# Edge counts from 16-bit keys, lanes first, and one product for attributes and squares

## The reference, cut to what matters

```
out_deg = segment_sum(ones, src, num_segments=12500)      # how many edges leave each node
h       = concatenate([x[row], edge_attr], axis=1)        # edge_attr: 400000 x 32
m       = h.mean(0)
v       = ((h - m) ** 2).mean(0)                          # batch norm over the edges
```

## Time and profile before

| what | value |
|---|---|
| median of three runs | 26533.92 us |
| the profiled execution, time | 26542.53 us |
| the profiled execution, span | 26540.7 us |
| VectorE busy, whole span | 58% |
| TensorE busy, whole span | 57% |
| GpSimd busy, whole span | 59% |

### The profile page before, as it was taken

The page is one execution under the profiler, slowest core; times in us unless marked ns, Lnnn a source line. Parts: engine busy times, 40 slices in busy tenths (PEclk is TensorE's granted clock), DMA queues, the critical chain, the costliest instruction groups (busy, mean ns, idle before and its releaser), DMA issues. The chain is left out here.

```text
span 26540.7 us, 456722 instructions
## 1 busy us (share of the span) xinstructions
PE 15258.6 (57%) x102440; PEld 9002.1 (34%) x102441; DVE 15401.4 (58%) x31597; ACT 5213.2 (20%) x13760; POOL 15770.5 (59%) x16798
## 2 busy tenths in 40 slices
PE   7555555566666689951000000024777777787777
PEld 5344444333333388920000000023333333333333
DVE  9666666656566644431111118985666666666666
ACT  4211111111111144410000000000222222222222
POOL 0377777677777744416777777721555555555554
PEclk9655555555555555555555555555888888888888
DMA  2466666433333345403333332212444444444444
GB/s 66 117 173 172 173 173 173 112 68 69 68 69 68 63 148 154 131 15 86 92 92 92 92 92 70 71 46 66 111 111 111 110 110 110 110 111 110 110 110 104
DMA packets 2864906, 2738.33 MB, mean 103 GB/s; under 512 B 1320271, under 2 KB 2226317, under 8 KB 2861906
## 3 DMA queue, kind: packets, MB, share of 16 engines
q1 hardware_dynamic: 2297486, 2308.45, 31.4%
q0 software_dynamic: 412544, 241.53, 6.1%
q10 hardware_dynamic: 153668, 172.93, 2.6%
HBM read 2173.30 MB, written 537.93 MB: 102 GB/s over the span
## 5 line engine op out<-in xcount | busy, mean ns | idle before, releaser
L2225 POOL DMA_INDIRECT rows_x<-x_table,index x3125 | 2974.6, 952 | 3538.4 <-DMA index<-in_src 2765.6
L742 POOL DMA_INDIRECT rows<-split_table,index x3125 | 2999.6, 960 | 1937.5 <-DMA index<-in_src 1008.2
L1624 POOL DMA_INDIRECT rows_dram<-rows,place_now x3125 | 3026.4, 968 | 1484.9 <-issue 952.3
L858 POOL DMA_INDIRECT rows<-x_table,index x3125 | 3279.8, 1050 | 1021.3 <-issue 952.1
L2339 DVE TENSOR_TENSOR second<-banks,h 128x768 f32<-128x768 f32 x2500 | 1944.8, 820 | 1597.8 <-PE banks L2494 1597.8
L1552 DVE TENSOR_REDUCE rows<-banks 128x108 f32<-128x324 f32 x1250 | 490.7, 434 | 3467.3 <-DMA rows_dram<-rows,place_now 3450.7
L1564 PE MATMUL banks<-row_pieces,hot_turned 128*128 x3125 | 394.1, 291 | 3604.6 <-DMA hot_turned<-turned_dram 3602.0
L2331 DVE TENSOR_TENSOR first<-banks,h 128x768 f32<-128x768 f32 x2500 | 1937.9, 818 | 259.3 <-issue 138.3
L550 PE MATMUL banks<-counts,low_turned 128*128 128x98 f32 x6250 | 1793.3, 435 | 80.3 <-ACT counts L538 47.3
L550 PEld LDWEIGHTS banks<-counts,low_turned 128*128 128x128 f32 x6250 | 1600.9, 314 | 205.4 <-issue 175.1
L2469 PE MATMUL banks<-u_turned,w_tensor 32*128 32x384 f32 (+1 forms) x10000 | 1565.0, 501 | 145.3 <-DVE second L2339 145.3
(11 more groups left out here) (480 smaller groups left out, 33841.6 us busy)
## 6 DMA issues: line engine op xcount, KB each, us to landing
key_row<-dst_rows SPq DMA_DIRECT2D x1250, 320.0 KB, 3.5
h<-hidden_dram SPq DMA_DIRECT2D x1250, 320.0 KB, 4.2
acc_moved<-dst_rows SPq DMA_DIRECT2D x625, 320.0 KB
src_row<-in_src_rows SPq DMA_DIRECT2D x625, 320.0 KB
hot_turned<-turned_dram SPq DMA_DIRECT2D x1250, 160.0 KB, 3.2
hot_dram<-onehot SPq DMA_DIRECT2D x625, 160.0 KB
turned_dram<-hot_turned SPq DMA_DIRECT2D x625, 160.0 KB
a_dram<-a ACTq DMA_DIRECT2D x625, 160.0 KB
```

Of the source, the lines that this page charges most:

```text
L742: nc.gpsimd.indirect_dma_start(out=m["rows"][j][:, t * SPLIT:(t + 1) * SPLIT], out_offset=None, in_=m["split_table"], in_offset=bass.Indir ...
L858: nc.gpsimd.indirect_dma_start(out=m["rows"][j][:, t * C2:t * C2 + F], out_offset=None, in_=m["x_table"], in_offset=bass.IndirectOffsetOnA ...
L1624: nc.gpsimd.indirect_dma_start(out=m["rows_dram"], out_offset=bass.IndirectOffsetOnAxis(ap=m["place_now"][j][:, t:t + 1], axis=0), in_=m[" ...
L2225: nc.gpsimd.indirect_dma_start(out=m["rows_x"][j][:, t * F:(t + 1) * F], out_offset=None, in_=m["x_table"], in_offset=bass.IndirectOffsetO ...
```

## The change

The edges' keys `low` get a bfloat16 copy, `low_half`, and the ramp is written out once as bfloat16 with each value five times in a row, `ramp_each`. Both operands and the result of the two comparisons are then bfloat16. The tiles `hot_low` and `hot_high` are laid out with the lanes innermost: value r, lane t is column 5*r + t. The comparison therefore runs over rows of five; the key is read as the same row of five again and again, the ramp and the result in one run. The counting products read one lane of such a tile, which is every fifth element, for the weights and for the moving operand.

The squares are written behind the attributes in one tile `attr[j]` of 320 columns, and one float32 product of ones with the 320 columns takes the place of the two with 160. Both sums lie in bank 1. The waits are as they were. Values 0 to 127 are exact in bfloat16.

```diff
@@ SyncE @@
-                    sp.dma_start(m["attr"][j][:, :], m["edge_attr"][:, bass.ds((SLOTS * i + j) * T * F, T * F)]
+                    sp.dma_start(m["attr"][j][:, 0:T * F], m["edge_attr"][:, bass.ds((SLOTS * i + j) * T * F, T * F)]
@@ ScalarE @@
-                    nc.scalar.square(m["attr_square"][j][:, :], m["attr"][j][:, :]).then_inc(s["squared"], 1)
+                    nc.scalar.square(m["attr"][j][:, T * F:], m["attr"][j][:, 0:T * F]).then_inc(s["squared"], 1)
@@ VectorE @@
             nc.vector.tensor_copy(m["ident_half"][:, :], m["ident"][:, :])
+            link(nc.vector.tensor_copy(m["low_half"][:, :], m["low"][:, :]))
+            by_lane = lambda tile: tile.rearrange("p (r t) -> p r t", t=T)
+            link(nc.vector.tensor_copy(by_lane(m["ramp_each"][:, :]), rep(m["ramp"][:, :], 2, T)))
             with dve.Fori(0, ITERS) as i:
                 for j in range(SLOTS):
                     dve.wait_ge(s["counted"][j], ONE + i)
                     cols = bass.ds((SLOTS * i + j) * T, T)
-                    nc.vector.tensor_tensor(cut(m["hot_low"][j][:, :], t=T), rep(m["low"][:, cols], 2, P),
-                                            rep(m["ramp"][:, :], 1, T), ALU.is_equal)
-                    nc.vector.tensor_tensor(cut(m["hot_high"][j][:, :], t=T), rep(m["high"][:, cols], 2, NB),
-                                            rep(m["ramp"][:, 0:NB], 1, T), ALU.is_equal).then_inc(s["hot"], 1)
+                    nc.vector.tensor_tensor(by_lane(m["hot_low"][j][:, :]), rep(m["low_half"][:, cols], 1, P),
+                                            by_lane(m["ramp_each"][:, :]), ALU.is_equal)
+                    nc.vector.tensor_tensor(by_lane(m["hot_high"][j][:, :]), rep(m["high"][:, cols], 1, NB),
+                                            by_lane(m["ramp_each"][:, 0:T * NB]), ALU.is_equal).then_inc(s["hot"], 1)
...
-            nc.vector.tensor_reduce(m["attr_sum"][:, F:2 * F], by_feature(m["ps"][2]), AX.X, ALU.add)
+            nc.vector.tensor_reduce(m["attr_sum"][:, F:2 * F], by_feature(m["ps"][1][:, T * F:]), AX.X, ALU.add)
@@ TensorE @@
-            for k in (1, 2):
-                nc.tensor.matmul(m["ps"][k][:, 0:T * F], m["zeros"][:, :], m["zero_row"][:, 0:T * F], start=True, stop=False,
-                                 skip_group_check=True)
+            nc.tensor.matmul(m["ps"][1][:, 0:2 * T * F], m["zeros"][:, :], m["zero_row"][:, 0:2 * T * F], start=True, stop=False,
+                             skip_group_check=True)
...
-                        mm = nc.tensor.matmul(m["ps"][3][:, t * NB:(t + 1) * NB], m["hot_low"][j][:, t * P:(t + 1) * P],
-                                              m["hot_high"][j][:, t * NB:(t + 1) * NB],
+                        mm = nc.tensor.matmul(m["ps"][3][:, t * NB:(t + 1) * NB],
+                                              m["hot_low"][j][:, :].rearrange("p (r t) -> p t r", t=T)[:, t, :],
+                                              m["hot_high"][j][:, :].rearrange("p (r t) -> p t r", t=T)[:, t, :],
                                               start=False, stop=False, skip_group_check=True)
                     mm.then_inc(s["counted"][j], 1)

                     pe.wait_ge(s["squared"], ONE + SLOTS * i + j + 1)
-                    nc.tensor.matmul(m["ps"][1][:, 0:T * F], m["ones"][:, :], m["attr"][j][:, :],
-                                     start=False, stop=False, skip_group_check=True)
-                    nc.tensor.matmul(m["ps"][2][:, 0:T * F], m["ones"][:, :], m["attr_square"][j][:, :],
+                    nc.tensor.matmul(m["ps"][1][:, 0:2 * T * F], m["ones"][:, :], m["attr"][j][:, :],
                                      start=False, stop=False, skip_group_check=True).then_inc(s["attr_used"][j], 1)
@@ tiles @@
-                m["attr"] = [inner.enter_context(nc.sbuf_tensor(f"attr{j}", [P, T * F], F32)) for j in range(SLOTS)]
-                m["attr_square"] = [inner.enter_context(nc.sbuf_tensor(f"attr_square{j}", [P, T * F], F32)) for j in range(SLOTS)]
+                m["attr"] = [inner.enter_context(nc.sbuf_tensor(f"attr{j}", [P, 2 * T * F], F32)) for j in range(SLOTS)]
+                sb("low_half", COLS, BF16, into=inner); sb("ramp_each", T * P, BF16, into=inner)
```

## The result

The changed kernel takes 26,400.8 us (median of six runs, 26,374.8 to 26,414.5), against 26,530.8 for the kernel before in the runs beside it: a ratio of 0.995, 95% interval 0.9937 to 0.9962. It is faster by 130 us, not by the 292 forecast. The time lies inside the wide range (26,222 to 26,478) and the sign is right, but it lies outside the forecast's own range (26,229 to 26,279), and the size is less than half of what was said.

The account below looks back on a forecast made before the run. VectorE was taken to bound the setup loop. Start 21.5, three slow steps 4.8, 622 x 0.84 = 522.5 and 0.5 end it at 549.3 us against 841.34: 292 less, median 26,242; range 26,222 to 26,478, own range 26,229 to 26,279.

Parts of the forecast that it names:

- What bounds the kernel, and what is late next: Setup loop: VectorE bounds it at 1.3135 us a step; once that is faster, TensorE sets the step, 0.83 us.
- Every fifth element in the counting products: Counting products reading weights and moving columns 10 bytes apart: zero to 0.035 us more a step, 0.045 to 0.052 a pair.
- a new bound between the two: Rival: VectorE packs only from even columns, or stepped columns stream at float32 rate; 1.02 us a step, 26,354 us; chance 0.27.
- SBUF Cachelines: Counting products: full rate needs two hits per 16-byte line, so a pair costs 0.056 us, a step 0.055 more, 26,276 us.
- TensorE's first steps: Start of the loop: three slow TensorE steps, 1.60 us apart, 4.8 us in all, would now show.
- The comparisons: VectorE's two comparisons per loop step, with all three operands bfloat16: 0.73 us a step, upper end 1.31.
- One product instead of two: Merging the loop's two float32 sums on TensorE: cost zero, at best 0.07 us less a step.
- The attributes' way: Loop's attribute transfer and squares on ScalarE, with the table load once in five steps: cover just holds, 0.01 us added.
- One-time terms: Two VectorE instructions ahead of the loop, a cast of 1.8 us and the ramp of 0.7 us, hidden by nothing.

Follow-up runs that it names:

- price rows: Changed kernel with 20 products for each pair of operand steps and five comparisons for each key pattern added behind the loop; run again, 26,218.1 us, ratio 0.9883.
- pairs kernel: Changed kernel with tiles back to lane after lane, each key written twice side by side and compared packed, both product operands in a row; 26,250.3 us, ratio 0.9891.

## Why the prediction was wrong

**What bounds the kernel, and what is late next** was right: the loop alone changed, VectorE stopped being the bound, TensorE took its place, and its step without stepped columns is the 0.83 us read from the earlier trace rows. Only the size of one term was off.

**The step that failed is "Every fifth element in the counting products".** It priced a pair at 0.045 to 0.052 us, by L1843 in the earlier trace rows, and in the step of 0.84 it stands at nothing. That row is a weight load, in float32, and both rows were taken at a granted clock of 0.50, where the loop has 1.00; the price rows show that a step of 5 adds nothing in the weights, while a pair with stepped moving columns takes 0.110. The only stepped row that the trace held was on the operand that doesn't matter, and the text took it as the nearest row for both. What was missing is 5 x (0.110 - 0.045) = 0.33 us a step. Less the 0.05 that the sums lost and what 0.84 held over 0.83, that is about the 0.26 between the 1.10 us of a step and the 0.84 taken; times 622 steps, it gives the 162 us by which the loop ended later than the forecast's 549.3.

The case stood among the rivals ("a new bound between the two"): columns at the float32 passes' rate, 0.082 a pair, 1.02 a step, 26,354 us. That the stepped columns stream slower was right; the rate taken was too small a price, by 0.028 a pair and 0.08 a step. The other half of that rival, that VectorE packs only from even columns, is ruled out by the price rows from columns 0, 1 and 5. The rival shared 0.27 with all else between 0.90 and 1.22, and a row of another operand was read as evidence against it.

The rule that was quoted from the Trainium skill ("Advanced Engine Details and Errata", SBUF Cachelines) does not hold for this operand: two hits on a line of 16 bytes were to be enough for full rate, yet at a step of 4, with just two columns on a line, a pair costs 0.089 us and not 0.045. As worked out in the prediction it gave 0.056 for a step of 5; measured were 0.110. Whether 16 bytes is the unit is open: up to a step of 8, the longest tried, the price goes with the bytes passed over.

The loop's start tells one thing more about that price:

```profile
21.81 0.54 DVE L440 TENSOR_TENSOR hot_low<-low_half,ramp_each 128x640 bf16<-128x640 bf16 x1
22.63 0.55 DVE L440 TENSOR_TENSOR hot_low<-low_half,ramp_each 128x640 bf16<-128x640 bf16 x1
...
23.72 0.75 PE L464 MATMUL banks<-hot_high,hot_low 128*128 128x98 bf16 x5
24.29 1.17 PE L471 MATMUL banks<-attr,ones 128*128 128x320 f32 x2
25.29 0.72 PE L464 MATMUL banks<-hot_high,hot_low 128*128 128x98 bf16 x5
```

The sum at 24.29 still takes 1.00 us to the next product, against 0.56 later, but the five stepped products before it take 0.57, as later. In the kernel before, the five took 0.41 in such a slow step (L462 at 21.25, L468 at 21.66) and 0.22 later. So what slows TensorE's first steps hardly touches the price of stepped columns. These steps were two, of 1.68 and 1.57 us, where the forecast had three of 1.60.

**The comparisons** were packed, as taken. Their price, 0.73 us a step, was 0.10 too low: rows of five add 0.06 to the larger tile and, by its size, some 0.04 to the smaller. While VectorE is ahead, at the loop's start, its step is 0.82 to 0.83 us (21.81 to 22.63), so by chance both engines need the same time in the step that was forecast; it cost nothing, since TensorE is slower. By the packed rate of the Trainium skill ("VectorE: DVE Perf Modes", the perf-mode tier table) the price rows agree: from start to start, 0.40 us where float32 needs 0.74. That rows of five lose a part of it was in no row of before.

**One product instead of two** was right at zero: 3 us in all where TensorE bounds the loop, nothing where VectorE does. **The attributes' way** held: ScalarE's table load delays a square, and no summing product waits for one, not even at 0.83 us a step. **One-time terms**: the two casts took 1.78 and 0.49 us, against 2.5 in all; the first comparison starts at 20.96 in place of 18.14.

## What to carry to other kernels

A layout that makes one engine fast is paid for by the engine that reads it: before the lanes are put innermost, price the reader's step, on the operand that is stepped. In a matmul the two operands have different prices: with 128 weights and 98 columns in bfloat16, a step of five elements was free in the weights and made a pair 2.5 times as dear in the moving columns. Where a packed comparison needs a repeated key, a key written twice gives the packed rate and leaves the reader its row: here that was worth 154 us, more than the change itself.

## What the runs showed that had not been expected

The kernel with the price rows took 147 us less than the changed kernel although it does more, and on a chip where the kernel before took 39 us more. It was run again:

> The changed kernel with the price rows behind the loop once more, for its whole time: it took 147 us less than the changed kernel although it does more, and the difference lay in the last stage, which no edit touches (7,808 against 8,034 us, TensorE's granted clock 0.88 against 0.86 there). If the place of the code or the moment at which the stage starts sets that, it is 200 us shorter again in every run; if it is chance, the runs scatter around the changed kernel's time plus 42 us (the setup's end at 773 against 731).

26,218.1 us, 0.9883 (0.9866 to 0.9899), and 186 us below the changed kernel beside it: not chance. Its L235 starts 42 us later, and its last stage, which no edit touches, takes 7,793 us from the first to the last gather of `rows_x`, against 8,034 in the changed kernel and 8,038 in the kernel before. Three more kernels ask whether TensorE's code, VectorE's code or the moment of the start does that, all on the pairs kernel.

```diff
+ for k in range(220): matmul(ps[2][:, 0:NB], low_pair[:, 0:P], low_pair[:, 0:NB])     # v2_pe_rows
+ for k in range(55): tensor_tensor(hot_low[k % 5], low_pair, high_pair, is_equal)     # v2_dve_rows
+ for k in range(6): tensor_copy(high_pair, high, twice each)                          # v2_delay
```

> The pairs kernel with 220 more products behind the loop, into a bank that nothing reads (added work, some 10 us). The price-row kernel's last stage was 226 us shorter than that of every other kernel, with the same instructions in it. If the place of TensorE's code sets that, the last stage takes some 7,800 us here and the whole some 215 us less than the pairs kernel, 26,035; if VectorE's code does, or the moment at which the stage starts, or none of them, the last stage takes 8,040 and the whole some 10 us more, 26,260.

> The pairs kernel with 55 more comparisons on VectorE behind the loop, into tiles that nothing reads any more (added work, some 24 us). If the place of VectorE's code sets the last stage's length, it takes 7,800 us and the whole some 200 us less than the pairs kernel; otherwise 8,040, and 24 us more.

> The pairs kernel with six long copies on VectorE behind the loop (added work, some 40 us, six instructions), so that every later stage starts 40 us later with its code almost where it was. If the moment of the start sets the last stage's length, it may change by as much as 200 us; if the code's place does, the last stage stays at 8,040 us and the whole is 40 us longer.

The gathers of the last stage (ns min/median/max, first and last start) in the pairs kernel, with the products, and with the delay:

```profile
L2227 POOL DMA_INDIRECT rows_x<-x_table,index x3125: 940/946/1053, 18108.2 to 26150.5; - x196
```

```profile
L2229 POOL DMA_INDIRECT rows_x<-x_table,index x3125: 940/946/1058, 18126.3 to 25946.0; - x196
```

```profile
L2229 POOL DMA_INDIRECT rows_x<-x_table,index x3125: 940/945/1060, 18173.7 to 26212.1; - x196
```

The stage takes 8,042 us in the pairs kernel, 7,820 with 220 products of TensorE put ahead of it, 8,038 with the delay and 8,037 with the comparisons. The wholes: 26,054.9 us with the products, 0.9817 (0.9801 to 0.9834), the fastest of all kernels here; 26,288.9 with the comparisons, 0.9902 (0.9885 to 0.9919); 26,308.4 with the delay, 0.9912 (0.9895 to 0.9928). So neither a start 65 us later nor more VectorE code does it. In all thirteen traces the stage takes 7,793 to 7,820 us in the three with more products on TensorE, which start it at 18,126, 18,309 and 18,337 us, and 8,032 to 8,066 in the ten others, which start it between 18,108 and 18,403. 220 more products on TensorE, whose results nothing reads, shorten a stage 17 ms later by 222 us, more than the change itself. The granted clock of TensorE over the stage is 0.88 in place of 0.86, which may be a cause or a result. That the place of TensorE's code in memory is what counts is the reading that is left, and it is argued only: its place was not moved without adding instructions. What it means for this case: a gain of half a per cent may come from a stage that the edit never touched, so the stages' own lengths have to be compared before a whole is put down to an edit. In the changed kernel they are the same as before, within 10 us each.
